# A two-layer graph network on one core: the source half of the projection made one node tile per batch of the target stage, the attention output on POOL, the bin counts inside the attention loop

## What is computed

```python
edge_index = jnp.stack([src, dst])
h = jnp.maximum(_layernorm(x, axis=-1), 0.0)
x = x + _L0_gnn_ref(h, edge_index, L0_gnn_W, L0_gnn_att_src, L0_gnn_att_dst, L0_gnn_bias)
h = jnp.maximum(_layernorm(x, axis=-1), 0.0)
x = x + _L1_gnn_ref(h, edge_index, edge_attr_64, L1_gnn_W1, L1_gnn_b1, L1_gnn_W2, L1_gnn_b2)
```

## Time and profile before

| | us |
|---|---|
| three runs | 6135.52, 6139.42, 6147.58 |
| median | 6139.42 |
| the profiled execution: its time | 6133.63 |
| its span, first to last instruction | 6131.8 |
| busy in the span: PE, DVE, POOL, ACT | 5318.2, 4156.3, 3563.1, 2679.5 |
| mean granted TensorE clock | 0.928 |

### The profile page before, as it was taken

How to read it: one execution, slowest core, us unless ns; L and a number is a source line. 1 busy time by engine, 2 the same in 40 slices (tenths; PEclk the granted TensorE clock), 3 DMA queues, 4 the chain that set the end, 5 groups by cost and what they waited for, 6 DMA issues and landing times.

```text
span 6131.8 us, 157219 instructions
## 1 busy us (share of the span) xinstructions
PE 5318.2 (87%) x36152; PEld 4148.2 (68%) x36153; DVE 4156.3 (68%) x13735; ACT 2679.5 (44%) x7281; POOL 3563.1 (58%) x4112
## 2 busy tenths in 40 slices
PE   3688888888888887899999898988987999999998
PEld 2466676766676763366666666666666888888887
DVE  5578787878787886555554545544545888888886
ACT  1455555555555553232222222222223555555554
POOL 1577777777777770177777777777774222222221
PEclk8688888889888885699999999999998999999999
DMA  5122222222222223598888898888984555555554
GB/s 160 41 52 52 52 53 52 53 52 52 53 52 53 52 49 108 167 264 262 256 250 260 249 261 252 256 255 250 260 250 147 161 159 161 161 160 162 159 160 125
DMA packets 785997, 924.85 MB, mean 151 GB/s; under 512 B 299677, under 2 KB 587709, under 8 KB 785792
## 3 DMA queue, kind: packets, MB, share of 16 engines
q1 hardware_dynamic: 644146, 595.14, 35.4%
q0 software_dynamic: 128960, 321.27, 17.6%
q10 hardware_dynamic: 12686, 6.51, 0.4%
HBM read 667.16 MB, written 255.39 MB: 150 GB/s over the span
## 4 chain that ended last, share of the span: by engine, by line
PE 47%; POOL 19%; issue 14%; DVE 10%; DVEq 3%; DMA 3%; ACT 2%; ACTq 1%; POOLq 0%; SPq 0%
POOL xr L430 17%; PE bank L1495 12%; PE bank L1358 10%; PE bank L1485 9%; PE bank L1289 3%; PE bank L1441 2%; PE bank L1439 2%; DMA xr<-arena 2%; DVE arena L883 2%; DVE arena L896 2%; POOL arena L402 2%; DVEq L216 2%; PE bank L1476 2%; DVE arena L799 2%; PE bank L1391 1%
## 5 line engine op out<-in xcount | busy, mean ns | idle before, releaser
L430 POOL DMA_INDIRECT xr<-arena x1612 | 1585.3, 983 | 727.8 <-issue 475.0
L402 POOL DMA_INDIRECT arena<-h_tab,arena x1612 | 1618.0, 1004 | 590.3 <-issue 482.7
L1358 PE MATMUL bank<-arena 128*128 128x136 f32 x6448 | 1280.3, 326 | 95.0 <-DVE arena L896 9.3
L607 ACT ACTIVATE arena<-bank 128x256 f32<-128x256 f32 x1612 | 583.3, 385 | 1481.2 <-PE bank L1441 963.5
L1358 PEld LDWEIGHTS bank<-arena 128*128 128x128 f32 x6448 | 950.0, 208 | 197.0 <-issue 88.8
L1441 PE MATMUL bank<-arena 128*128 128x256 f32 x3224 | 982.0, 386 | 107.4 <-DVE arena L1108 104.7
L498 ACT ACTIVATE arena<-bank 128x256 bf16<-128x256 bf16 x1612 | 616.6, 383 | 975.2 <-PE bank L1289 882.6
L1439 PE MATMUL bank<-arena 128*128 128x256 f32 x3224 | 1006.8, 394 | 17.2 <-DVE arena L1093 16.4
L444 POOL CAST arena<-arena 128x256 bf16<-128x256 f32 x856 | 342.9, 401 | 1059.7 <-DVE arena L1169 1056.8
L1495 PE MATMUL bank<-arena 128*128 128x257 f32 x3424 | 885.3, 381 | 0.0
L896 DVE TENSOR_TENSOR arena<-arena,bank 128x272 f32 x1612 | 692.2, 429 | 211.0 <-PE bank L1358 168.2
(11 more groups left out here) (261 smaller groups left out, 6568.8 us busy)
## 6 DMA issues: line engine op xcount, KB each, us to landing
arena<-xr SPq DMA_DIRECT2D x428, 514.0 KB, 3.7
arena<-q_tab SPq DMA_DIRECT2D x1612, 128.0 KB
arena<-in_edge_attr SPq DMA_DIRECT2D x61, 832.0 KB
arena<-rel_tab SPq DMA_DIRECT2D x124, 224.0 KB
arena<-h_tab,arena POOLq DMA_INDIRECT x1612
xr<-arena POOLq DMA_INDIRECT x1612
arena<-rel_tab SPq DMA_DIRECT2D x124, 192.0 KB
xr<-arena SPq DMA_DIRECT2D x26, 514.0 KB, 8.5
```

Of the source, the lines that this page charges most:

```text
L402: pool.indirect_dma_start(G[:, q, t, :], None, h_tab, bass.IndirectOffsetOnAxis(ap=idx[:, q, t:t + 1], axis=0)).then_inc(sem(f"gath{q}"), 16)
L430: pool.indirect_dma_start(xr, bass.IndirectOffsetOnAxis(ap=pos[:, q, t:t + 1], axis=0), Rb[:, t, :], None).then_inc(sem(f"scat{m}"), 16)
L1358: last = pe.matmul(PSB[3 + t % 2][:, k * H * MW:(k + 1) * H * MW], OH[:, (t + 2 * q) % 4, k * P:(k + 1) * P], flat(msg[:, t, :, :]), start ...
```

## The change

- **Target stage.** PE makes the source half of one node tile in each of the batches 0 to 47 and in batch 60 (`source_part`): a 128x256 product with the turned rows of the tile (`hcol`, copied by ACT at tile 15 from `h2T`, which now holds all 49 tiles) and the product with `b1`, at tile 21. ACT rounds it at tile 22, DVE takes the rest into `resd` at tile 24, ACT rounds that after tile 25, and DVE takes the last part at tile 3 of the next batch. PE waits for DVE's first rest before tile 0 of the next batch counts into the same bank.
- **Node stage.** PE multiplies with the target half only, 256 columns, two tiles to a bank; ACT copies two tiles at once (`q_rows`). The four operations that make the attention output run on POOL (`t_step`), two rounds' buffers ahead of DVE. DVE takes the denominators of all 49 tiles at once. DVE's and PE's work for the places of batch 0 stands between the rounds, and SP loads batch 0's windows after round 4's Q.
- **Attention.** Counts and runs are made in batch 58, the pair table in batch 59; the filler blocks are written from there on, no more one by one; h and x of rounds 0 and 1 are loaded in the loop.

The core of the diff, SP first, then POOL, ACT, DVE and PE:

```diff
             def load_nodes(c):
-                sp.dma_start(hs[:, c % 2, :, :], rows(h_tab, c)[:, :, 0:D]).then_inc(sem(f"hs_in{c % 2}"), 16)
+                h, v = (hs0, xi0) if c < 2 else (hs, xi)
+                if c >= 2:
+                    sp.wait_ge(sem(f"hs_in{c % 2}"), 32 * (c // 2))
+                sp.dma_start(h[:, c % 2, :, :], rows(h_tab, c)[:, :, 0:D]).then_inc(sem(f"hs_in{c % 2}"), 16)
...
+            sp.wait_ge(sem("hx_used"), NCH)
+            load_nodes(0)
+            load_nodes(1)
             sp.wait_ge(sem("rend_ready"), 1)
-            sp.wait_ge(sem("zl_ready"), 2)
+            sp.wait_ge(sem("zl_ready"), 3)
+            sp.wait_ge(sem("filled"), 16 * NFILL)
             for c in range(NCH):
-                sp.wait_ge(sem("x1_ready"), c + 1)
-                sp.dma_start(rows(x1_tab, c), x1c).then_inc(sem("x1_out"), 16)
-                if c + 2 < NCH:
-                    load_nodes(c + 2)
                 fill_ends(c)
...
+            sp.wait_ge(sem("rend_ready"), 2)
+            sp.dma_start(pb_tab.rearrange("(p j) -> p j", p=P), pbi).then_inc(sem("pb_out"), 16)
+            sp.wait_ge(sem("acc_done"), 1 + NB * (BT + 1))
+            sp.wait_ge(sem("expanded"), NB * BT)
+            load_nodes(2)
+            load_nodes(3)
...
+            for c in range(NCH):
+                sp.wait_ge(sem("x1_ready"), c + 1)
+                sp.dma_start(rows(x1_tab, c), x1c[:, c % 2, :, :]).then_inc(sem(f"x1_out{c % 2}"), 16)
+                if c >= 2 and c + 2 < NCH:
+                    load_nodes(c + 2)
+                sp.wait_ge(sem("hi_ready"), (c + 1) * NQ)
+                sp.dma_start(rows(q_tab, c), Qst[:, c % 2, :, :]).then_inc(sem(f"q_out{c % 2}"), 16)
+                if c == 4:
+                    sp.wait_ge(sem("node_prep"), 2)
+                    load_windows(0, 0, first=True, more="next")
...
+            for c in range(NCH):
+                a = acc[:, c * NC:(c + 1) * NC, :].rearrange("p n (h m) -> p n h m", h=H)
+                t1, h = tt[:, c % 2, :, :], hs0 if c < 2 else hs
+                if c >= 2:
+                    pool.wait_ge(sem("h2_ready"), c - 1)
+                pool.wait_ge(sem(f"hs_in{c % 2}"), 32 * (c // 2 + 1) + (16 if c == NCH - 1 else 0))
+                M.tensor_tensor(hv(t1), hv(h[:, c % 2, :, :]), wide(a[:, :, :, DH + 1]), ALU.mult).then_inc(sem("t_step"), 1)
+                pool.wait_ge(sem("t_step"), 3 * c + 1)
+                M.tensor_tensor(hv(t1), hv(t1), a[:, :, :, 0:DH], ALU.add).then_inc(sem("t_step"), 1)
+                pool.wait_ge(sem("t_step"), 3 * c + 2)
+                if c == 0:
+                    pool.wait_ge(sem("node_prep"), 1)
+                M.tensor_tensor(hv(t1), hv(t1), wide(rec[:, c * NC:(c + 1) * NC, :]), ALU.mult).then_inc(sem("t_step"), 1)
+                pool.wait_ge(sem("t_step"), 3 * c + 3)
+                M.tensor_tensor(t1, t1, biasB.unsqueeze(1).to_broadcast([P, NC, D]), ALU.add).then_inc(sem("t_ready"), 1)
...
+                    if part is not None and t == 15:
+                        A.activation(hcol.unsqueeze(1), h2T[:, bass.ds(part, 1), :], ACT.Copy).then_inc(sem("part_in"), 1)
+                    if part is not None and t == 22:
+                        act.wait_ge(sem("pq_ps"), NCH * NQ + part + 1)
+                        A.activation(Pt[:, bass.ds(part, 1), 0, :], PSB[7][:, HID:], ACT.Copy).then_inc(sem("hi_ready"), 1)
...
+                if part is not None:
+                    act.wait_ge(sem("res_ready"), part + 1)
+                    A.activation(Pt[:, bass.ds(part, 1), 1, :], resd, ACT.Copy).then_inc(sem("mid_ready"), 1)
...
+                act.wait_ge(sem("pq_ps"), u + 1)
+                A.activation(flat(Qst[:, c % 2, 2 * k:2 * k + n, :]), PSB[2 + u % 3][:, 0:n * HID], ACT.Copy).then_inc(sem("hi_ready"), 1)
...
+                    if t == 16 and table == "runs":
+                        dve.wait_ge(sem("counted"), NT)
+                        V.tensor_copy(cntT, PSB[6][:, 136:136 + NT]).then_inc(sem("cntT_ready"), 1)
+                    if t == 16 and table == "pairs":
+                        pair_table()
...
+            a4 = acc[:, 0:NT, :].rearrange("p n (h m) -> p n h m", h=H)
+            link(V.tensor_tensor(den, a4[:, :, :, DH], a4[:, :, :, DH + 1], ALU.add))
+            link(V.tensor_scalar(den, den, 1e-30, None, ALU.max))
+            V.reciprocal(rec, den).then_inc(sem("node_prep"), 1)
+
+            def node(c):
+
+                t1, x1, v = tt[:, c % 2, :, :], x1c[:, c % 2, :, :], xi0 if c < 2 else xi
+                dve.wait_ge(sem("t_ready"), c + 1)
+                dve.wait_ge(sem(f"hs_in{c % 2}"), 32 * (c // 2 + 1) + (16 if c == NCH - 1 else 0))
+                if c >= 2:
+                    dve.wait_ge(sem(f"x1_out{c % 2}"), 16 * (c // 2))
+                V.tensor_tensor(x1, t1, v[:, c % 2, :, :], ALU.add).then_inc(sem("x1_ready"), 1)
...
+            def low_part(n):
+
+                dve.wait_ge(sem("mid_ready"), n + 1)
+                V.tensor_tensor(Pt[:, bass.ds(n, 1), 2, :], resd.unsqueeze(1), Pt[:, bass.ds(n, 1), 1, :], ALU.subtract).then_inc(sem("lo_ready"), 1)
...
+                        if t == 24 and part is not None:
+                            dve.wait_ge(sem("hi_ready"), NCH * NQ + part + 1)
+                            V.tensor_tensor(resd.unsqueeze(1), PSB[7][:, HID:].unsqueeze(1), Pt[:, bass.ds(part, 1), 0, :], ALU.subtract).then_inc(sem("res_ready"), 1)
...
+            for c in range(NCH):
+                node(c)
+                if c == 0:
+                    for m in range(2):
+                        rank(0, m)
+                        own(0, 0, m)
+                if c == 1:
+                    rank(0, 2)
+                    own(0, 0, 2)
+                    total(0)
+                if c == 2:
+                    reduced(0)
+                    places(0, 0)
+                    dve.wait_ge(sem("d0_in"), 16)
...
-                    pe.matmul(PSB[2 + n % 6][:], h2T[:, j, :], flat(w1n), start=True, stop=False)
-                    pe.matmul(PSB[2 + n % 6][:, 0:HID], ones[0:1, :], b1r, start=False, stop=True).then_inc(sem("pq_ps"), 1)
-
+                for k in range(NQ):
+                    u = c * NQ + k
+                    if u >= 3:
+                        pe.wait_ge(sem("hi_ready"), u - 2)
+                    for j in range(2 * k, min(2 * k + 2, NC)):
+                        last = pe.matmul(PSB[2 + u % 3][:, (j % 2) * HID:(j % 2 + 1) * HID], h2T[:, c * NC + j, :], w1n[:, 1, :], start=True, stop=True)
+                    last.then_inc(sem("pq_ps"), 1)
...
+            def source_part(n, r):
+
+                pe.wait_ge(sem("run_ready"), r + 1)
+                pe.wait_ge(sem("part_in"), n + 1)
+                pe.matmul(PSB[7][:, HID:], hcol, w1n[:, 0, :], start=True, stop=False)
+                pe.matmul(PSB[7][:, HID:], ones[0:1, :], b1r, start=False, stop=True).then_inc(sem("pq_ps"), 1)
...
+                        if t == 0 and parts is not None:
+                            pe.wait_ge(sem("res_ready"), parts)
+                        if t == 21 and part is not None:
+                            source_part(part, r)
...
+            with pe.Fori(1, NT // 2) as i:
                 for q in range(2):
-                    targets(2 * i + q, q)
-            targets(NB - 2, 0)
+                    targets(2 * i + q, q, part=2 * i + q, parts=2 * i + q)
+            with pe.Fori(NT // 2, NB // 2 - 1) as i:
+                for q in range(2):
+                    targets(2 * i + q, q, parts=NT - 1)
+            targets(NB - 2, 0, part=NT - 1)
```

More of the change, by code:

```diff
@@ L1338, in _, with batch @@
             chain_carry(0)
[L1340 removed]
+            def batch(b, q, ahead2=True, ahead1=True, first=False, table=""):
                 if ahead2:
@@ L1370, in _, with node @@
             batch(1, 1)
-            with pe.Fori(1, NB // 2 - 1) as i:
+            with pe.Fori(1, NB // 2 - 2) as i:
                 for q in range(2):
                     batch(2 * i + q, q)
+            batch(NB - 4, 0, table="runs")
+            batch(NB - 3, 1)
             batch(NB - 2, 0, ahead2=False)
             batch(NB - 1, 1, ahead2=False, ahead1=False)
-            pe.wait_ge(sem("cntT_ready"), 1)
-            pe.matmul(PSB[6][:, 264:264 + NT], ones, cntT, start=True, stop=True).then_inc(sem("cnt_ps"), 1)
-            for c in range(NCH):
+            def node(c):
                 pe.wait_ge(sem("h2_ready"), c + 1)
+                if c:
+                    pe.wait_ge(sem("h2T_ready"), c)
                 for j in range(NC):
```

308 lines of the change are left out of this document (141 added, 167 removed).

## The result

| | before | changed |
|---|---|---|
| median, us | 6138.7 (4 runs, 6135.52 to 6147.58) | 6211.12 (4 runs, 6210.01 to 6223.49) |
| ratio | 1 | 1.012 (95%: 1.0103 to 1.0138) |
| span of the profiled execution | 6131.8 | 6207.9 |
| first to last gather (attention) | 2144.3 | 2150.4 |
| DVE's first operation of the node stage to the second main product | 224.3 | 105.4 |

The forecast was 6005 in a range of 5984 to 6032. The node stage gave back 119 us (in the table it begins in the kernel before at L985, behind the operations on the counts; in the forecast's measure, from attention's last add-up, it is 226.4 and 104.9). The target loop took 186.5 us more. The rest is the node stage's start, 11 us later, 5 of them already at the first gather. These make 78.6; the two profiled spans differ by 76.1.

A forecast was written before the change was run, and what follows sets the result against it. POOL was taken to bound attention and target loops, PE the source loop and, at half clock, the node stage. 226.4 - 90.1 - 1.5 - 1 = 134 us off 6139.4 gave 6005, range 5984 to 6032.

The forecast's parts named there:

- the part on the target loop: Target loop: the source part's PE, DVE and ACT work lies in cover; 1 us charged, for first batches and shared ports.
- Rival 4: Target loop: the part's PE-DVE-ACT round trip catches landings and starves POOL; costs 225 us, total 6230; chance 0.03.
- PE's free time: Target loop: PE has 3.3 us a batch free; the part's two products take 0.43 each, together 0.86.
- rival 3: Target loop: PE's free time isn't free, each part costs POOL 0.86; 42 us, total 6047; chance 0.06.
- The node stage: Between attention and target loop: from attention's last add-up to the first main product, 90.1 us against 226.4.
- The head: Node stage, first round: 7.3 us on POOL, then 7.5 on DVE to the normalised rows.
- the tail: Node stage, end: last round 10.4 us on PE and last copy 0.5, together 10.9.
- POOL's operations: Node stage: four attention output operations a round on POOL, 1.75 us each (bounds 1.09 and 2.4), 7.3 a round with waits.
- Rival 2: Node stage: POOL slow at 2.4 an operation, total 6010; or standing still for DVE on shared ports, 6021; ports chance 0.11.
- SP's loop: Node stage: SP issues loads behind Q rows; 32.0 us for three rounds, 10.7 each, holding rounds 4 to 6.
- rival 1: Node stage: the clock rises, PE saves some 4.7 us a round; total 5991; chance 0.10.
- Attention: Attention loop: small DVE operations on counts and tables in batches 58 and 59 cost 1.5 us (0 to 4).

The follow-up runs named there:

- a_shift8: Changed kernel with 16 passed waits (8 instructions) on DVE just ahead of the target loop over batches with parts; 6018.21 us, ratio 0.9789.
- eight-fold kernel: Changed kernel with the 8-instruction shift, the PE products of every source part made eight times; 6592.0 us, ratio 1.0739.
- a_best: Changed kernel, attention output back on DVE, four batches an iteration in DVE's attention loop, target loop's DVE code in three blocks without padding; 6019.93 us, ratio 0.9802.
- b_body12_shift: Kernel before with 12 passed waits ahead of each batch in DVE's target loop and 214 ahead of that loop; 6261.68 us, ratio 1.0187.

## Why the prediction was wrong

**The step that failed** is in the part on the target loop: "DVE gets two 256-wide operations, ACT three copies, all in the same cover. [...] I take 1 us, for the first batches". I had priced what the new instructions do and not that they lengthen a loop, whose code then lies over one block more. At the place where the program happens to put it, DVE's body was fetched anew at each of 22 back edges, at 8.5 us each: 187 us. Without that the same kernel takes 6013 to 6018, within the range. That instructions have to be fetched was in none of the five cases.

**Rival 4** named a total of 6230, 19 us over the measured one, for another reason, a round trip with landings (its loss in the loop was 225, the measured one is 186.5). The round trip cost nothing: a_shift8 has every hop of it at 2069.8. Even the direction was right by luck. A price that nearly fits is no proof of a mechanism.

**PE's free time.** Two errors, both to the same side: the pair costs 1.15, not 0.86 (0.52 and 0.63 where 0.43 was taken for each), and 2.0 us a batch are free, not 3.3. For one part a batch the conclusion held (hidden), for three it would not. From there on an added us of PE costs POOL one, as rival 3 (given 0.06) has it, and with the clock of the eight-fold kernel more.

**The node stage**: 104.9 in the forecast's measure against 90.1. That is still under the 110 that I had named as the limit. The head took 20.2 in place of 14.8, the six rounds to the last normalised rows 76.4 in place of 64.4, and the tail 8.4 in place of 10.9.

- *POOL's operations.* 1.75 was taken. The first four of the changed kernel:

```profile
2350.71 2.14 POOL L447 TENSOR_TENSOR arena<-arena 128x896 f32<-128x896 f32 x1 [52.25 <-DVE arena L946]
2352.93 1.93 POOL L449 TENSOR_TENSOR arena<-arena 128x896 f32<-128x896 f32 x1
2354.94 1.80 POOL L453 TENSOR_TENSOR arena<-arena 128x896 f32<-128x896 f32 x1
2356.81 2.22 POOL L455 TENSOR_TENSOR arena<-arena 128x896 f32<-128x896 f32 x1
```

  They range from 1.69 to 3.02. The mean of the 28 is 2.15. The Trainium skill (GPSIMD Engine Reference, Performance versus the Vector engine) gives 2.6 cycles an element at 1.2 GHz, by which one operation is an estimated 1.94 us: nearer than mine.
- *The ports.* Beside them DVE's own were slow. The four of L1078 take 1.6 us together in a_best, where POOL is idle. In the changed kernel:

```profile
2351.28 1.69 DVE L1050 TENSOR_SCALAR arena<-arena 128x196 f32<-128x196 f32 x1
...
2354.30 7.03 DVE L1078 TENSOR_TENSOR arena<-arena 128x294 bf16<-128x294 bf16 x4
```

  DVE's sum with x, ready to go at 2359.0, started at 2363.1, behind L1078 and L1084, and the first normalised rows were there at 20.2 us, not at 14.8. Rival 2 let POOL stand still for DVE; here both are slowed, and DVE more. On contention for SBUF the trace agrees with that page (Specifications).
- *SP's loop.* 32.0 us for three rounds was the forecast, 37.3, 35.9 and 41.2 were measured. Two things were missing: SP itself takes 1.3 and 2.0 us to issue a round's two loads, and the Q copies of a round stand on ACT behind the square of the next (round 3's first copy starts at 2409.7, its second at 2419.3, behind round 4's square at 2418.4), which waits for that round's load. SP in the changed kernel, round 4's load:

```profile
2395.69 0.38 SPq L327 DMA_DIRECT2D q_tab<-arena  x1
2396.11 0.56 SPq L323 DMA_DIRECT2D x_tab<-arena  x1
2396.72 1.32 SPq L257 DMA_DIRECT2D arena<-h_tab  x1
2398.09 1.96 SPq L259 DMA_DIRECT2D arena<-in_x  x1
```

- *PE.* It was not at half clock throughout, nor the bound. Windows of the changed kernel, columns as in rows 1:

```profile
2351.00:2429.00 78.00, 37.04 (x155) 27.73 (x156) 59.70 (x58) 21.27 (x40) 52.45 (x24) 0.61 0.53 142
2429.50:2442.50 13.00, 5.54 (x27) 4.09 (x25) 4.80 (x7) 3.23 (x7) 7.44 (x4) 1.00 0.60 178
```

  So what rival 1 names, a higher clock in this stage, came in part, and its gain did not: DVE, POOL and the loads set the pace, and PE was busy for less than half of the first 78 us. PE's work was also taken too large. A round has 10.4 in the forecast and 5.4 to 9.2 in the trace (from the transposes to the last product; 7.6 in the last round, which is why the tail is short), since a 256-wide product was priced as the one with one row, 1.08 us; in round 0, at half clock, it takes 0.75.
- *The kernel before.* Its stage was put down to PE, but the working adds up to 194 of 226 us. Each of rounds 1 to 6 begins with a wait for DVE, and 16 us lie between the last round's products and the first main product:

```profile
2382.15 1.76 PE L1383 MATMUL bank<-arena 128*128 128x128 f32 x7 [3.03 <-DVE arena L1017]
```

- *Right*: the two loads of rounds 0 and 1 on time, the window rows off the path, and the first scatter 108 us earlier.

**Attention**: 1.5 us taken. It stays open: first to last gather is 2144.3, 2149.7 and 2157.4 in three kernels whose attention loop is the unedited one, and 2149.7 to 2163.4 in those with the edit (on the usual chips; a_shift8 alone had 2152.7 once and 2157.6 the other time).

**Source loop**: unchanged, as forecast.

## What to carry to other kernels

A loop in a program has a size in instructions on each engine, and a place. Before work is moved into a loop, count the engine's body: here DVE's loops over three blocks of 128 ran without a fetch and those over four or more did not, and then the engine stood still at every back edge, for 3 us in one loop and for 10 to 11 in another. In a profile look for idle time put down to "issue" at the loop's period, and for packets of the instruction queue inside the loop; a few idle instructions ahead of it tell in one run whether it is that. And where SP's queue carries loads and stores of a pipeline, put the load that starts a later round ahead of the store that only ends one.

## What the runs showed of the hardware

- **Instruction blocks.** The Trainium skill (Runtime: NRT & Kernel Launch, Instruction fetch mechanics) says that a taken branch to a page outside the two that are held forces a fetch, with pages of 256 instructions. That a loop too large is fetched again at the branch is what the traces show. The size is another: the packets of q14 carry 8.2 KB, DVE's loops over three blocks of 128 were held, a shift by 128 kept the stalls (2280.7), and one by 8 removed them (2069.8).
- **The same five packets cost DVE different stalls.** At a back edge it was 3 us in attention (DMA share 0.24), and in the target loop 9.9 in b_body12_shift and 10.7 in the changed kernel (0.86 in the 30 us ahead of the place shown). That the traffic of the queues makes the difference fits, but no run changed it alone.
- **The clock follows a stall.** Behind an idle stretch of PE of 5.1 us the clock was at 0.50 (1.2 GHz) for 13 us, with a second stretch of 5.2 in them, and so, for 7 to 17 us, in every iteration. In a_shift8 the loop ran at 1.00 (2.4 GHz) from 2500 to 4520.
- **The clock can fall without idle time.** In the eight-fold kernel it went to 0.50 after 37 us with PE busy for 35.86, at the end of sixteen products, half of which have one row. Whether it is these products that let it fall, no run shows.
- **A product with one row is no shorter.** At full clock the one-row product of the part, 256 wide, takes 0.63 us from start to start (3155.08 to 3155.71 in the changed kernel), and main products of that width with 128 rows stand 0.43 apart.
